# Attention on one Trainium2 core: the order of two TensorE steps, probabilities times values and the outputs' transposes

## What is computed

```python
x1 = _ln(x) * (scale1 + 1.0) + shift1
qkv = (x1 @ mat_qkv_w.T + qkv_bias).reshape(B, L, 3, H, hd)
q, k, v = [jnp.transpose(qkv[:, :, i], (0, 2, 1, 3)) for i in range(3)]
q = _l2norm(q) * jnp.exp(jnp.minimum(scale_mul, MAX_SCALE_MUL))
k = _l2norm(k)
probs = jax.nn.softmax(jnp.einsum('bhqd,bhkd->bhqk', q, k), axis=-1)
o = jnp.einsum('bhqk,bhkd->bhqd', probs, v)
o = jnp.transpose(o, (0, 2, 1, 3)).reshape(B, L, C)
x = x + (o @ proj_w.T + proj_b) * gamma1
...
# then the feed-forward part (gelu, 256 -> 1024 -> 256) and the linear attention
```

## Time and profile before

| | us |
|---|---|
| median of 3 runs | 1211.41 (1210.38 to 1213.47) |
| the profiled execution | 1209.6 |
| its span, first to last instruction | 1207.9 |
| attention pass, first turn_o to the last instruction | 76.8 to 449.7 |
| of it, 46 steps between the turn_o that start at 125.44 and 392.72 | 267.28 |

### The profile page before, as it was taken

The page is one execution under the profiler, slowest core; times in us unless marked ns, Lnnn a source line. Parts: engine busy times, 40 slices in busy tenths (PEclk is TensorE's granted clock), DMA queues, the critical chain, the costliest instruction groups (busy, mean ns, idle before and its releaser), DMA issues. The chain is left out here.

```text
span 1207.9 us, 33635 instructions
## 1 busy us (share of the span) xinstructions
PE 1080.3 (89%) x10050; PEld 762.3 (63%) x10050; DVE 923.9 (76%) x2403; ACT 778.0 (64%) x2077; POOL 861.1 (71%) x1087
## 2 busy tenths in 40 slices
PE   4677898888888857999999999996999999999996
PEld 3355666666666643666776677664666666666664
DVE  6578999999999747555546556426999999999984
ACT  2468888888888734454544445534777777777774
POOL 4488899999999745366665757542577777777777
PEclk8799999999999987999999999998999999999999
DMA  7696789898897842001000010100011111111112
GB/s 250 173 185 101 109 112 115 113 116 111 112 115 116 117 70 62 19 18 36 17 28 24 17 35 18 34 19 1 19 42 42 42 56 42 40 56 43 39 57 84
DMA packets 184508, 84.83 MB, mean 70 GB/s; under 512 B 109824, under 2 KB 183168, under 8 KB 184448
## 3 DMA queue, kind: packets, MB, share of 16 engines
q1 hardware_dynamic: 156048, 58.10, 29.8%
q10 hardware_dynamic: 28400, 25.99, 7.4%
HBM read 41.58 MB, written 8.65 MB: 42 GB/s over the span
## 5 line engine op out<-in xcount | busy, mean ns | idle before, releaser
L1182 PE MATMUL f_ps_h<-f_x_split,w_fc 128*128 128x512 bf16 x768 | 173.2, 383 | 2.1 <-DVE f_biases L1305 1.2
L1155 PE MATMUL f_ps_y<-w_fc,f_h_split 128*128 128x256 bf16 x1536 | 172.7, 273 | 1.4 <-DVE f_branch L1274 1.4
L1155 PEld LDWEIGHTS f_ps_y<-w_fc,f_h_split 128*128 128x128 bf16 x1536 | 150.2, 98 | 22.5 <-issue 1.7
L1282 DVE TENSOR_TENSOR f_h_split<-f_h,f_h_split 128x512 bf16<-128x512 f32 x64 | 64.0, 1003 | 104.2 <-ACT f_h L1141 104.2
L678 POOL TENSOR_TENSOR e_split<-e_full,e_split 128x1024 bf16<-128x1024 f32 x64 | 136.6, 2135 | 8.9 <-ACT e_full L750 8.9
L1516 ACT ACTIVATE l_z_t<-l_ps_yt,shift,scale 128x64 f32<-128x64 f32 x256 | 82.7, 403 | 91.8 <-PE l_ps_yt L1582 64.7
L1140 ACT ACTIVATE f_h_split<-f_ps_h,columns 128x512 bf16<-128x512 f32 x128 | 89.1, 696 | 66.3 <-POOL f_h_split L1101 36.3
L1182 PEld LDWEIGHTS f_ps_h<-f_x_split,w_fc 128*128 128x128 bf16 x768 | 75.6, 99 | 88.6 <-issue 3.0
L827 PE MATMUL ps_qk<-w_qkv,x_split 128*128 128x512 bf16 x384 | 100.4, 400 | 13.7 <-DVE norms L859 10.8
L1101 POOL TENSOR_TENSOR f_h_split<-f_h,f_h_split 128x512 bf16<-128x512 f32 x64 | 79.8, 1256 | 36.5 <-ACT f_h L1141 36.5
L1633 PE MATMUL l_ps_qv<-w_qvk,l_x_split 128*128 128x512 bf16 x384 | 95.2, 384 | 4.7 <-DVE l_v_split L1737 4.6
(11 more groups left out here) (184 smaller groups left out, 3102.3 us busy)
## 6 DMA issues: line engine op xcount, KB each, us to landing
k_stack<-qk_t SPq DMA_DIRECT2D x192, 64.0 KB, 4.0
q_stack<-qk_t SPq DMA_DIRECT2D x96, 128.0 KB, 4.5
v_pairs<-v_split SPq DMA_DIRECT2D x128, 66.0 KB, 3.3
gain<-gammas SPq DMA_DIRECT2D x64, 128.0 KB, 3.0
f_gain<-gammas ACTq DMA_DIRECT2D x32, 256.0 KB, 4.3
l_gate<-in_cond ACTq DMA_DIRECT2D x128, 64.0 KB, 2.6
out<-x_all ACTq DMA_DIRECT2D x16, 512.0 KB, 2.9
x_all<-in_x SPq DMA_DIRECT2D x13, 512.0 KB, 8.7
```

What stands on the lines that cost most here:

```text
L1155: last = pe.matmul(ps_y[:, i], h_split[a][:, hs, f, i * P:(i + 1) * P], m.w_fc2[:, ws, f], start=(f == 0 and k == 0), stop=(f == F_CHUNKS ...
L1182: last = pe.matmul(ps_h[f % 4][:], m.w_fc1[:, ws, c, f * P:(f + 1) * P], x2_split[a][:, xs, c], start=(k == 0 and c == 0), stop=(k == 2 an ...
```

## The change

One line: in TensorE's list, `(9, probs_v)` now stands ahead of `(10, turn_o)`. The functions, their waits and the lists of the other engines are the same.

```diff
-            pipeline(pe, [(5, turn_qk), (8, scores), (10, turn_o), (9, probs_v), (11, project), (3, qkv),
+            pipeline(pe, [(5, turn_qk), (8, scores), (9, probs_v), (10, turn_o), (11, project), (3, qkv),
                           (1, turn_x)])
```

## The result

| | before | after |
|---|---|---|
| median of 5 runs, us | 1212.67 (1210.38 to 1215.05) | 1222.53 (1221.41 to 1223.80) |
| profiled execution, and its span | 1209.6, 1207.9 | 1221.4, 1219.7 |
| 46 steps, us (one step) | 267.28 (5.81) | 275.30 (5.98) |

The changed kernel takes 1.0081 times as long, 95% interval 1.0065 to 1.0098: 0.8% slower.

The account below looks back on a forecast made before the run. VectorE, 96% busy, sets 5.81 us a step; the new loop adds 0.15 in each of 46 steps (6.9), 1.0 around them, 1.8 in the run-down: 1209.6 + 9.7 = 1219.3, median 1.8 higher: 1221 us, range 1213 to 1231.

Parts of the forecast that it names:

- the closed loop: One-step chain e_lo, probs_v, turn_o, o_hi, x1_high, x1_low, normalise, e_lo: 5.96 us a step against 5.81.
- e_lo's end to probs_v: Hand-over from GpSimd to TensorE: 0.06 us at positions 2 and 3, 0.24 at 0 and 1, mean 0.15.
- probs_v to turn_o: On TensorE, start to start across probs_v's 24 matmuls: 0.75 us, bounds 0.70 and 0.91.
- turn_o to o_hi: TensorE to idle ScalarE, start to start: 0.47 us, perhaps 0.04 more on average for separate wait instructions.
- o_hi to e_lo's end: From o_hi's start on ScalarE to the end of e_lo on GpSimd: 4.55 us, bounds 4.55 and 4.70.
- The ends: Outside the 46 steps: four more steps on either side, +1.0 us, and the run-down, +1.8 us.
- the run-down: End of the attention pass: last e_lo 1.17 us later, the step before losing perhaps half of that, +1.8 us.
- Rival 1: VectorE keeps the pace and the attention pass its time but for the run-down: 1210 to 1214 us, chance 0.15.
- the list of signs: Expected in the profile after: step 5.9 to 6.0 us, VectorE under 95% busy, waiting at L904 for ScalarE.
- worth of the removal: nothing: Ending TensorE's wait at turn_o for modulate, 24.1 us in all, gains nothing while VectorE sets the pace.
- Rival 2: Faster: earlier probs_v ends v_hi's wait for v_pairs, at most 5.9 us, 1206 us; chance 0.06.
- Rival 3: Much slower: o_low's delay returns to turn_o through modulate, 0.4 to 0.6 us a step, 1232 to 1243 us; chance 0.05.

Follow-up runs that it names:

- e7: Changed kernel with qk_lo on VectorE for the queries alone, the low half of the keys left out: 1222.39 us, 5.98 us a step.
- e6: Kernel before with qk_lo on VectorE for the queries alone, the low half of the keys left out: 1208.23 us, 5.74 us a step.
- e10: Kernel before with the low half of the keys (VectorE) and of the second sequence's exponentials (GpSimd) left out: 1204.60 us, 5.75 us a step.
- e13: Kernel before with 12 of probs_v's matmuls done a second time, behind turn_o and ahead of project: 1228.32 us, 6.10 us a step.
- e9: Changed kernel with the low half of the second sequence's exponentials left out of e_lo on GpSimd: 1208.06 us, 5.79 us a step.

## Why the prediction was right, point by point

**The number.** 1221 us were forecast, 1222.53 measured, inside 1213 to 1231; +9.7 us against +9.9 between the medians and +11.8 between the profiled executions. The forecast case, the closed loop, was the one that came. The size of the ends, as shown below, was luck in part.

**The loop's terms.** Every one of the four was taken from a row of before, and the trace of after has them as follows:

| term | forecast | after |
|---|---|---|
| e_lo's end to probs_v | 0.06 (positions 2, 3), 0.24 (0, 1) | 0.05, 0.25 |
| probs_v to turn_o | 0.75 | 0.76, 0.74 |
| turn_o to o_hi | 0.47, and 0.04 on average for separate wait instructions | 0.45, and 0.53 |
| o_hi to e_lo's end | 4.55 | 4.56, and 4.63 |
| step | 5.96 | 5.98 |

The one small part that was not foreseen is the last 0.07 at two positions. It stands between x1_high and x1_low, whose starts are 0.57 us apart at positions 0 and 1 (247.34 and 247.91 above) and 0.49 at the others (259.06 and 259.55): the 4.55 had been read at a position of the second kind and taken for all. The other terms came out 0.02 shorter together; what is left, 0.02 to 0.03 a step, is the difference between 8.0 and 6.9 us in the 46 steps. The 0.25 and the 0.53 stand at positions whose wait has an instruction of its own, and the 0.05 and the 0.45 at the others, in step after step. No run took one of these instructions away, so that they are the cause is argued, not shown. The Trainium skill ("Perfetto Trace Analysis", section Identifying Dependency Chains) says that such instructions may be put in; the program has them, as at L789, and the trace shows the longer hand-overs where they stand.

**The ends.** Forecast were 1.0 us for the steps around the window and 1.8 for the run-down, 2.8 together. Measured are -0.5 from the first e_lo to tile 7's turn_o (56.52 us where it was 57.02) and +2.4 from tile 53's turn_o to the end of the pass. The sum is near; the reasoning behind it did not hold.

The 1.8 was built on a last e_lo that starts 1.17 us later. It starts at 449.50, 47.57 us after tile 53's turn_o; before it was 440.31, 47.59 after it. Nothing was lost up to there: the probs_v ahead of it came 1.17 us earlier, at 446.83, 44.90 after tile 53's turn_o against 46.07 before. All of the 2.4 us stands behind the last e_lo's end, 9.74 us to the end of the pass where it was 7.27:

```profile
449.50 2.12 POOL L678 TENSOR_TENSOR e_split<-e_full,e_split 128x1024 bf16<-128x1024 f32 x1 [2.04 <-ACT e_full L750]
...
451.68 1.50 PE L794 MATMUL ps_o<-v_pairs,e_split 128*128 128x66 bf16 x24 [2.92 <-POOL e_split L678]
...
452.99 0.67 PE L783 MATMUL ps_x<-ident,o_full 128*128 128x128 f32 x2
...
453.67 1.44 PE L773 MATMUL ps_v<-w_proj,o_t 128*128 128x256 bf16 x6
...
458.62 1.48 PE L773 MATMUL ps_v<-w_proj,o_t 128*128 128x256 bf16 x6
...
460.64 0.72 POOL L663 TENSOR_TENSOR x_all<-x_all,branch 128x256 f32<-128x256 f32 x1 [1.50 <-DVE branch L879]
```

and in the kernel before the last row of the pass:

```profile
448.98 0.72 POOL L663 TENSOR_TENSOR x_all<-x_all,branch 128x256 f32<-128x256 f32 x1 [0.76 <-DVE branch L879]
```

TensorE's granted clock is 0.53 from 451.62 to 455.15 us and 0.50 from 458.40 to 460.20, that is nearly all at 1.2 GHz, and 1.00 in the whole of that stretch before. The matmuls show it: probs_v to turn_o takes 1.31 us and not 0.76, turn_o to project's L773 0.68 and not 0.36, L773 itself 1.44 and 1.48 and not 0.82. These make 2.15 us together, an estimate from the rows, so most of the 2.4 is the lower clock. TensorE had been idle for 2.92 us ahead of 451.68, waiting for e_lo; the longest such wait in that stretch before is 1.57 us. That the longer wait brought the lower clock is likely, and not shown. The forecast of the run-down had no clock in it.

**Rival 1** (VectorE keeps the pace) fell: VectorE at 94%, with a wait at L904, as the list of signs said; e7 took 11.9 us of its work away and the window did not move. The rule that the engine of the highest occupancy is the one to improve (the Trainium skill, "Perfetto Trace Analysis", section Identifying the Most-Contended Engine) would have said no change here; the measurement decides against it. 4 to 5% less VectorE work brought 0.3% before the change and nothing after. In the order before, the engine's name is not enough: 3.61 of the loop's 5.65 us are VectorE's own stages, from residual to modulate, but the work that e6 left out stands outside them.

**What the reasoning had wrong.** "VectorE, and not TensorE, sets the step" was only half true of the kernel before. Its steps are, at three of four positions, a loop through both engines, 5.65 us at the shortest and 5.75 on average, in which TensorE's turn_o, probs_v and project stand between two stages of VectorE (e6, e10, e13). So "worth of the removal: nothing" had the right size and the wrong reason: the removal opened a loop that did set the pace, but VectorE's work of 5.59 us lies close behind it, and the new loop is 0.23 us longer on average (5.98 against 5.75). e9, where that new loop is shortened, takes 5.79 us a step against the 5.81 of before. The rows of before could have told: at 253.45 turn_o has just been released by modulate, and the earlier trace rows has TensorE waiting for VectorE in 41 of 46 steps; two engines that hand each other work in every step are a loop, also where one of them shows no wait. Rival 2 (faster) was put on the DMA waits of v_hi; they did shrink, from 5.9 to 0.7 us, and nothing came of it. The loop through project was the other thing that the change removed; what opening it is worth with nothing left out, no run shows.

**Rival 3** (the delays add up) fell too: the four positions take the length of the loop (6.14, 6.14, 5.81 and 5.81 us) and nothing beside it.

## What to carry to other kernels

Where engines run one hand-ordered list per step, the pace can be, as in both orders here, the longest chain of waits that closes on itself in one step, and not the busiest engine. A reordering has to be read as a change of such loops: which one does it open, and does a stage with a late input now stand ahead of one whose result starts a long chain. The length of the new loop can be summed from rows of the old trace, hand-over by hand-over, taking each term from a place where that hand-over is the last to come, and at each position of the loop body. A pass's end wants its own look: there the clock of TensorE can be another.

An engine at 96% with no wait in the trace can still be held by a loop of the same length: take a little of its work away and see whether the step follows. A dose of harmless work, put ahead of and behind the suspected place, shows in one number whether a stage is inside the loop (0.37 of 0.38 us) or outside it (0.03).

## What the runs showed of the hardware

Hand-overs took longer at the loop positions where the wait has an instruction of its own: by 0.20 us between e_lo and probs_v (0.25 against 0.05 us), by 0.08 us between turn_o and o_hi (0.53 against 0.45) and by 0.08 us between x1_high and x1_low (0.57 against 0.49, start to start). At two of four loop positions that made the loop 0.33 us longer (6.14 against 5.81 us) with the same work.

At the end of the changed attention pass, after an idle stretch of 2.92 us, TensorE was granted 0.53 of its clock for 3.5 us, and the 24 matmuls of probs_v took 1.50 us where they take 0.92 in the steady steps, granted 1.00.
